# Products with the values issued two quads at a time, with a ring of three probability buffers and v biased in its operand

## The reference

```python
# cross attention, 16 heads of width 16, no scaling of the scores
q = decoded @ Wq.T + bq            # decoded = layernorm(x)
k = encoded @ Wk.T + bk
v = encoded @ Wv.T + bv
qk = einsum('bhqd,bhkd->bhqk', q, k)
attn = softmax(qk, axis=-1)        # nan in qk -> -inf, nan in attn -> 0
v = where(isnan(v), 0, v)
z = einsum('bhqk,bhkd->bhqd', attn, v)
x = x + layernorm(z + decoded) * gamma + beta
# mixture of experts: 8 experts, the best 2 for each row
z = layernorm(layernorm(x)) * ln_g + ln_b
w = top-2 of softmax(z @ rW + rb), normalised
x = x + layernorm(x) + sum over e of w[e] * (gelu(z @ W1[e] + b1[e]) @ W2[e] + b2[e])
```

## Time and profile before

| | us |
|---|---|
| median of three runs | 853.96 (852.0 to 855.2) |
| profiled execution | 848.4 |
| its span in the trace | 846.7 |
| attention pipeline in its steady state | about 55 to 528 of the span |
| PE busy | 752.9 (89%) |
| DVE busy | 655.0 (77%) |
| ACT busy | 534.6 (63%) |
| POOL busy | 553.3 (65%) |

### The profile page before, as it was taken

The page is one execution under the profiler, slowest core; times in us unless marked ns, Lnnn a source line. Parts: engine busy times, 40 slices in busy tenths (PEclk is TensorE's granted clock), DMA queues, the critical chain, the costliest instruction groups (busy, mean ns, idle before and its releaser), DMA issues.

```text
span 846.7 us, 26238 instructions
## 1 busy us (share of the span) xinstructions
PE 752.9 (89%) x8056; PEld 587.9 (69%) x8057; DVE 655.0 (77%) x1827; ACT 534.6 (63%) x1412; POOL 553.3 (65%) x610
## 2 busy tenths in 40 slices
PE   3489999999999999999999997655797798999994
PEld 2356777777777777777777775444686697999994
DVE  7398998998998998998989997993457865555562
ACT  2246787888888888888878885443363354554551
POOL 5424877777778777777778685333655466676773
PEclk9999999999999999999999999755899899999998
DMA  8765576676676676776776766611243233443441
GB/s 208 140 156 120 123 167 151 158 179 155 157 180 152 155 180 140 178 162 149 174 163 152 188 138 168 205 19 52 43 71 44 46 58 65 68 69 51 66 65 18
DMA packets 152791, 104.43 MB, mean 123 GB/s; under 512 B 68656, under 2 KB 147852, under 8 KB 152608
## 3 DMA queue, kind: packets, MB, share of 16 engines
q1 hardware_dynamic: 132598, 77.03, 40.0%
q0 software_dynamic: 11776, 16.15, 11.5%
q10 hardware_dynamic: 8362, 10.57, 4.3%
HBM read 36.65 MB, written 17.33 MB: 64 GB/s over the span
## 4 chain that ended last, share of the span: by engine, by line
PE 74%; DVE 12%; DMA 4%; issue 4%; POOL 3%; ACT 1%; DVEq 1%; ACTq 1%; POOLq 0%; SPq 0%
PE pj L863 10%; PE s_row L967 10%; PE pj L832 9%; PE s_row L877 9%; PE zt L908 9%; PE s_t L896 9%; PE pj L978 5%; PE zt L978 4%; DVE negmax L1332 3%; PE pj L850 3%; DMA q_stack<-q_part 1%; PE tr L916 1%; PE pj L955 1%; PE tr L932 1%; DVE p_t L1337 1%
## 5 line engine op out<-in xcount | busy, mean ns | idle before, releaser
L1332 DVE TENSOR_REDUCE negmax<-s_row 100x1 f32<-100x361 f32 x512 | 251.3, 523 | 30.3 <-PE s_row L877 23.9
L1155 ACT ACTIVATE p_t<-s_t 128x400 f32<-128x400 f32 x384 | 188.6, 501 | 56.4 <-PE s_t L896 50.1
L877 PE MATMUL s_row<-stack_x,q_stack 125*128 125x361 bf16 x512 | 132.3, 320 | 12.2 <-DVE negmax L1332 5.3
L703 POOL DMA_INDIRECT out_x<-index_space,idx_s x57 | 93.2, 1634 | 72.3 <-DVE index_space L1440 35.9
L896 PE MATMUL s_t<-q_stack,stack_x 128*128 128x100 bf16 x1536 | 128.8, 212 | 9.3 <-ACT p_t L1155 8.6
L896 PEld LDWEIGHTS s_t<-q_stack,stack_x 128*128 128x128 bf16 x1536 | 93.4, 99 | 55.4 <-issue 23.1
L967 PE MATMUL s_row<-w_qkv,v_aug 128*128 128x128 f32 x912 | 118.2, 285 | 12.7 <-DVE v_aug L1427 12.6
L967 PEld LDWEIGHTS s_row<-w_qkv,v_aug 128*128 128x128 f32 x912 | 111.9, 200 | 15.8 <-DVE v_aug L1427 14.4
L1337 DVE TENSOR_SCALAR p_t<-p_t 128x1200 f32<-128x1200 f32 x128 | 102.3, 799 | 6.8 <-ACT p_t L1155 5.6
L863 PE MATMUL pj<-w_qkv,ct 128*128 128x256 f32 x384 | 106.4, 400 | 0.2 <-ACT k_rest L1083 0.2
L1141 ACT ACTIVATE w_qkv<-s_row,b_k 128x128 f32<-128x128 f32 x228 | 65.0, 368 | 63.7 <-PE s_row L967 63.6
(11 more groups left out here) (233 smaller groups left out, 1431.9 us busy)
## 6 DMA issues: line engine op xcount, KB each, us to landing
stack_x<-k_part SPq DMA_DIRECT2D x192, 192.0 KB, 3.8
q_stack<-q_part SPq DMA_DIRECT2D x186, 64.0 KB, 2.0
ct<-in_ctx_t SPq DMA_DIRECT2D x32, 361.0 KB, 4.9
stack_x<-in_w ACTq DMA_DIRECT2D x8, 512.0 KB, 6.4
w_s<-in_w ACTq DMA_DIRECT2D x14, 256.0 KB, 3.1
zscr<-zn SPq DMA_DIRECT2D x32, 100.0 KB
z_in<-zscr SPq DMA_DIRECT2D x32, 100.0 KB
zf_d<-zf_s SPq DMA_DIRECT2D x32, 100.0 KB
```

The costliest lines, as they stand in the source:

```text
L703: pool.indirect_dma_start(out_rows[0:n], bass.IndirectOffsetOnAxis(idx_s[:, k.slot:k.slot + 1], 0), ys[:, k.slot, :], None, bounds_check=n ...
L877: nc.tensor.matmul(s_row[h % 2][:, 0:KEYS], q_stack[0:MROW, b.slot, h, :], k_stack[0:MROW, b.slot, h, 0:KEYS], start=True, stop=True).then ...
L1155: nc.scalar.activation(p_t[:, quad % 2, kt, :], s_t[g % 2][:, 0:4 * Q], ACT.Exp).then_inc(exp_done, 1)
L1332: v.tensor_reduce(negmax[:, b.slot, h:h + 1], s_row[h % 2][0:Q, 0:KEYS], AXIS.X, ALU.max, negate=True).then_inc(max_done, 1)
```

## The change

`values` is called twice in a row: quads 0 and 1 together, in slot 0 of the iteration after the batch's own, and quads 2 and 3 together in slot 6. Quad 0 so moves from slot 9 to slot 0, and quad 2 from slot 3 to slot 6; quads 1 and 3 stay. The wait for the guard stands only at the first of a pair, and is for both quads. `p_t` gets a third buffer and the exponentials of a quad wait for the values of the quad three back in place of two back. `v_raw` goes: the bias is added straight into `v_aug` (rows of 16 words, 32 apart) and the cleaning works in place; the wait for the old values of that slot moves from the cleaning to the bias. `ys` moves to `p_t` and small routing tables to `k_rest`, to make room.

```diff
+def ring(b, quad):
+    return (b.slot + quad) % 3
-        v_raw = sb(es, "v_raw", [128, KT * H, DH])
-        p_t = sb(es, "p_t", [128, 2, KT, 4 * Q])
+        p_t = sb(es, "p_t", [128, 3, KT, 4 * Q])
...
-            v_raw[0:Q].rearrange("q n d -> q (n d)"), (LATE, LATE, LATE, 2 * B, 4 * B, 2 * B, 2 * B, (NT - NF) * E, NT - NF))
+            k_rest[0:Q].rearrange("q c k -> q (c k)"), (LATE, LATE, LATE, 2 * B, 4 * B, 2 * B, 2 * B, (NT - NF) * E, NT - NF))
...
-            ys, idx0, idx1, slot_c, second = carve(idx_at, (2 * D, NT, NT, NT, NT))
+            idx0, idx1, slot_c, second = carve(index_space, (NT, NT, NT, NT))
+            ys = p_t[:].rearrange("p r k n -> p (r k n)")[:, 0:2 * D].rearrange("p (s d) -> p s d", s=2)
...
-                    pe.wait_ge(p_ready, G * b.index + quad + 1)
+                    if quad % 2 == 0:
+                        pe.wait_ge(p_ready, G * b.index + quad + 2)
...
-                                                    p_t[0:n, quad % 2, kt, j * Q:j * Q + Q], start=(kt == 0), stop=(kt == KT - 1))
+                                                    p_t[0:n, ring(b, quad), kt, j * Q:j * Q + Q], start=(kt == 0), stop=(kt == KT - 1))
...
-                        if n.valid() and g % KT == 0:
+                        if n.valid() and g in (KT, 3 * KT):
+                            values(n, g // KT - 1)
                             values(n, g // KT)
...
-                        after(act, pv_done, G * b.index + quad - 1)
-                    nc.scalar.activation(p_t[:, quad % 2, kt, :], s_t[g % 2][:, 0:4 * Q], ACT.Exp).then_inc(exp_done, 1)
+                        after(act, pv_done, G * b.index + quad - 2)
+                    nc.scalar.activation(p_t[:, ring(b, quad), kt, :], s_t[g % 2][:, 0:4 * Q], ACT.Exp).then_inc(exp_done, 1)
...
                 def values_biased(b, last):
-                    after(dve, v_ready, b.index)
+                    after(dve, pv_done, G * (b.index - 2))
...
-                        v.tensor_tensor(v_raw[:, 0:2 * H, :].rearrange("p (t h) d -> p t (h d)", t=2), pj[1][:, :].rearrange("p (t n) -> p t n", t=2),
-                                        bias2, ALU.add).then_inc(v01_biased, 1)
+                        v.tensor_tensor(v_aug[:, b.slot, 0:2 * H, 0:DH].rearrange("p (t h) d -> p t h d", t=2),
+                                        pj[1][:, :].rearrange("p (t h d) -> p t h d", t=2, d=DH), bias2, ALU.add).then_inc(v01_biased, 1)
...
                 def values_cleaned(b):
-                    after(dve, pv_done, G * (b.index - 2))
...
-                    v.scalar_tensor_tensor(v_aug[:, b.slot, :, 0:DH], v_raw[:], 0.0, v_raw[:], ALU.max, ALU.min).then_inc(v_ready, 1)
+                    biased = v_aug[:, b.slot, :, 0:DH]
+                    v.scalar_tensor_tensor(biased, biased, 0.0, biased, ALU.max, ALU.min).then_inc(v_ready, 1)
...
-                    v.tensor_scalar(p_t[:, quad % 2], p_t[:, quad % 2], 0.0, None, ALU.max).then_inc(p_ready, 1)
+                    v.tensor_scalar(p_t[:, ring(b, quad)], p_t[:, ring(b, quad)], 0.0, None, ALU.max).then_inc(p_ready, 1)
...
                 def result(k):
...
+                    if k.known and k.index == 0:
+                        dve.wait_ge(pv_done, G * B)
```

More of the change, by code:

```diff
@@ L476, in build @@
             q_stack = sb(att, "q_stack", [128, 3, H, QPAD], BF16)
-            index_space = sb(att, "index_space", [128, KT * D])
+            index_space = sb(att, "index_space", [128, 4 * NT])
             negmax = sb(att, "negmax", [Q, 3, H])
@@ L538, in build @@
             base = per_expert(drow[:])
-            idx_at = index_space
-            ys, idx0, idx1, slot_c, second = carve(idx_at, (2 * D, NT, NT, NT, NT))
-            ys = ys.rearrange("p (s d) -> p s d", s=2)
+            idx0, idx1, slot_c, second = carve(index_space, (NT, NT, NT, NT))
+            ys = p_t[:].rearrange("p r k n -> p (r k n)")[:, 0:2 * D].rearrange("p (s d) -> p s d", s=2)
             idx_t = [idx0, idx1]
@@ L1310, in values_biased @@
                 def values_biased(b, last):
-                    after(dve, v_ready, b.index)
+                    after(dve, pv_done, G * (b.index - 2))
                     if last:
                         dve.wait_ge(v2_done, b.index + 1)
-                        v.tensor_tensor(v_raw[:, 2 * H:3 * H, :].rearrange("p h d -> p (h d)"), pj[0][:, 0:D],
-                                        bv_s[:, :], ALU.add).then_inc(v2_biased, 1)
+                        v.tensor_tensor(v_aug[:, b.slot, 2 * H:3 * H, 0:DH], pj[0][:, 0:D].rearrange("p (h d) -> p h d", d=DH),
+                                        bv_s[:, :].rearrange("p (h d) -> p h d", d=DH), ALU.add).then_inc(v2_biased, 1)
                     else:
                         dve.wait_ge(v01_done, b.index + 1)
-                        bias2 = bv_s[:, :].unsqueeze(1).broadcast_to([128, 2, D])
-                        v.tensor_tensor(v_raw[:, 0:2 * H, :].rearrange("p (t h) d -> p t (h d)", t=2), pj[1][:, :].rearrange("p (t n) -> p t n", t=2),
-                                        bias2, ALU.add).then_inc(v01_biased, 1)
+                        bias2 = bv_s[:, :].rearrange("p (h d) -> p h d", d=DH).unsqueeze(1).broadcast_to([128, 2, H, DH])
+                        v.tensor_tensor(v_aug[:, b.slot, 0:2 * H, 0:DH].rearrange("p (t h) d -> p t h d", t=2),
+                                        pj[1][:, :].rearrange("p (t h d) -> p t h d", t=2, d=DH), bias2, ALU.add).then_inc(v01_biased, 1)
                 def values_cleaned(b):
-                    after(dve, pv_done, G * (b.index - 2))
                     dve.wait_ge(v2_biased, b.index + 1)
                     dve.wait_ge(v01_biased, b.index + 1)
-                    v.scalar_tensor_tensor(v_aug[:, b.slot, :, 0:DH], v_raw[:], 0.0, v_raw[:], ALU.max, ALU.min).then_inc(v_ready, 1)
+                    biased = v_aug[:, b.slot, :, 0:DH]
+                    v.scalar_tensor_tensor(biased, biased, 0.0, biased, ALU.max, ALU.min).then_inc(v_ready, 1)
                 def row_max(b, h):
```

## The result

The changed kernel is slower: 881.68 us in the median of 6 runs (879.68 to 886.24), against 852.98 us (850.0 to 855.84, 6 runs) for the kernel before. The ratio is 1.0349, with a 95% interval of 1.0321 to 1.0376. Predicted were 877.5 us, in a range of 866 to 888. The profiled execution took 881.81 us, with a span of 880.1.

The account below looks back on a forecast made before the run. PE's stream bounds the kernel, but a closed PE-DVE-ACT chain would set the iteration: 28 x 0.82 = 23.0 us plus 0.5 for the tail, 848.4 to 871.9 profiled, so 877.5 us against the 853.96 median; range 866 to 888.

Parts of the forecast that it names:

- the step that was under-sized: Other two iterations of a loop turn: assumed to lose the same 0.82 us as the one worked out.
- What the pairing removes: Values on PE: a lone quad costs 0.76 us, a second one 0.52, so a pair saves 0.24, two 0.48 an iteration.
- First place, head 7: Slot 4: with quad 2 gone from this stretch, PE's row scores of head 7 wait some 0.7 us for maximum 5.
- Second place, step 8: Slot 11: PE waits 0.80 us for exponential 6, with quad 0 gone from slot 9 and the old slot 8 wait gone.
- the second account: Cross-check of an iteration: PE's own work 14.82 us plus waits of 0.70 and 0.80 makes 16.32.
- The sum of an iteration: Closed chain PE to DVE and back twice: legs add to 16.33 us against 15.51, 0.82 more an iteration.
- The signs that I named: Profile after: L1319 repeats every 16.3 us, PE about 92% busy, DVE's idle time up about 0.8 us an iteration.
- The remaining edits at nothing: Guard wait, third buffer, bias with gaps, cleaning in place: taken as 0; bias between -0.05 and +0.1 us an iteration.
- The tail: Last batch: quad 2 right before quad 3 at half clock, last z up to 1.0 us later; taken 0.5, range 0 to 2.
- That no wait takes the place of the saving: Rival: entries and exits are saved without new waits, 14.82 us an iteration, 835 us; chance 0.06.
- that only one does: Rival: only head 7 or only step 8 waits, giving 854 to 857 us; chance 0.05.
- That back to back saves nothing: Rival: the second quad is held up like a lone one, 1.30 us more an iteration, 891 us; chance 0.06.

Follow-up runs that it names:

- Experiments 3 and 6: 3: changed kernel with only quads 2 and 3 paired, 864.03 us; 6: changed kernel with maxima of heads 4 and 5 over 181 of 361 keys, 871.93 us.
- experiment 4: The changed kernel with ACT's copy of the maxima moved from slot 8 to slot 9, behind exponential 6: 872.68 us, ratio 1.0222.
- experiment 1: The changed kernel with the pairing alone undone, the four quads standing one by one again: 853.35 us, ratio 1.0016.
- experiments 2 to 5: Changed kernel with only quads 0 and 1 paired, 862.45 us; only 2 and 3, 864.03; maxima copy in slot 9, 872.68; also z steps in slot 9, 864.71.
- experiments 4 and 5: Changed kernel with ACT's copy of the maxima in slot 9: 872.68 us; the same plus DVE's three z steps in slot 9: 864.71 us.
- both versions of 8 to 11: Quads 1 and 2 paired in slot 3, quad 0 in slot 11: 848.79, 849.83 us; quads 0 and 1 paired, maxima copy and z steps in slot 9: 848.56.
- their control: The version with quads 1 and 2 paired, but quad 1 alone in slot 0 and all other slots the same: 853.25 us, ratio 1.0017.
- experiment 8: The changed kernel with quads 1 and 2 paired in slot 3, quad 0 alone in slot 11, some ACT and POOL steps moved: 848.79 us, ratio 0.9956.

## Why the prediction was right, point by point

The forecast was 23.5 us more, the medians differ by 28.7. The mechanism is the one on record; the sum is short by 5 us, and the point on the step that was under-sized says where.

- **What the pairing removes.** Right. A block of 48 records lasts 1.24 us, to the digit 0.72 + 0.52.
- **First place, head 7.** Right in its mechanism and in when head 7 starts: 0.07 behind maximum 5. Right too in how long PE stands in all: from the scores at 307.84 to the row scores at 308.87 it takes 1.03 us where it took 0.56 (307.24 to 307.80), and 0.24 more inside the pair, together 0.71. Wrong in where: I put it all at the row scores, and most of it went earlier, at the router's transpose (308.46), of which 0.28 is put down to ACT, a wait that I hadn't looked for. It is beside the chain, since head 7 can't start sooner in any case. Experiments 3 and 6 show this leg.
- **Second place, step 8.** Right: 0.54 us idle for exponential 6 (step 8 starts 0.88 us after step 7 where it took 0.18, so 0.70 later in all), and the guard next behind it, as experiment 4 shows. The size I gave, 0.80, took the wait in slot 8 for gone. It grew instead to 0.77 - 0.47 = 0.30 us: the maximum of head 12 now starts late (DVE waits 0.31 us for its row score, at 314.76), and head 15 feels that. It is again beside the chain. Counted from start to start, PE stands 0.71 + 0.30 + 0.70 = 1.71 us in this iteration; the second account had 1.50, for an iteration that turned out 0.27 shorter than this one.
- **The sum of an iteration.** The iteration on which I worked gives 16.33; its fellow in the trace after, the next behind the one shown, takes 340.59 - 324.24 = 16.35. That is no balance of errors, since its legs agree one by one. Head 7 to head 12 is 5.01 us (worked out: 5.00), head 12 to the end of exponential 6 is 3.71 (3.73), and from there to the values it is 0.34 (0.32). Head 12, step 8 and the start of its wait are in these rows:

```profile
330.88 0.47 PE L880 MATMUL s_row<-stack_x,q_stack 125*128 125x361 bf16 x2
...
334.65 0.35 PE L899 MATMUL s_t<-q_stack,stack_x 128*128 128x100 bf16 x4 [0.42 <-ACT p_t L1160]
```

- **The signs that I named.** L1324 repeats every 16.48 us in the mean, as forecast to 0.2. PE's busy share is 94.1 to 94.6%, not 92 (and the prediction's own terms, 14.82 of 16.33, would make 91); why it is higher isn't shown. DVE's idle time grew from 9.4% of 15.65 us to 12.7% of 16.6, which is 0.6 us an iteration and not 0.8.
- **The step that was under-sized** is "I take the same difference for them", for the other two iterations of a loop turn. A turn took 337.63 - 290.69 = 46.94 us before and takes 340.59 - 290.75 = 49.84 now, 0.97 an iteration. These are the starts, of the kernel before and then of the changed one:

```profile
290.69 0.69 DVE L1319 TENSOR_TENSOR v_raw<-pj,bv_s 128x512 f32<-128x512 f32 x1 [0.36 <-PE pj L863]
...
337.63 0.69 DVE L1319 TENSOR_TENSOR v_raw<-pj,bv_s 128x512 f32<-128x512 f32 x1 [0.36 <-PE pj L863]
```

```profile
290.75 0.69 DVE L1324 TENSOR_TENSOR v_aug<-pj,bv_s 128x512 f32<-128x512 f32 x1 [0.36 <-PE pj L866]
...
340.59 0.69 DVE L1324 TENSOR_TENSOR v_aug<-pj,bv_s 128x512 f32<-128x512 f32 x1 [0.36 <-PE pj L866]
```

I had picked the iteration with most slack. In the one before it exponential 6 ended later against step 8; this row of ACT and this of PE are from the kernel before:

```profile
300.27 0.51 ACT L1155 ACTIVATE p_t<-s_t 128x400 f32<-128x400 f32 x1
```

```profile
301.14 0.72 PE L908 MATMUL zt<-p_t,v_aug 128*32 128x100 f32 x24
```

  Exponential 6 ends at 300.78, and step 8 starts 0.27 before the values, at 300.87: 0.09 us of room, against 0.22 in the iteration I used. So the chain of this iteration comes out 0.13 longer against what PE took, 0.95 us more; it took 1.03 more (324.24 - 307.62 = 16.62, before 306.28 - 290.69 = 15.59). The third iteration has the loop's branch. It stands in front of the values of slot 0, and now also right behind a wait. Before the change:

```profile
331.26 0.50 ACT L1155 ACTIVATE p_t<-s_t 128x400 f32<-128x400 f32 x1
```

```profile
331.70 0.52 PE L896 MATMUL s_t<-q_stack,stack_x 128*128 128x100 bf16 x8
332.31 0.91 PE L908 MATMUL zt<-p_t,v_aug 128*32 128x100 f32 x24
333.14 0.35 PE L896 MATMUL s_t<-q_stack,stack_x 128*128 128x100 bf16 x4
```

  And in the changed kernel:

```profile
301.27 0.35 PE L899 MATMUL s_t<-q_stack,stack_x 128*128 128x100 bf16 x4 [0.52 <-ACT p_t L1160]
301.97 1.24 PE L912 MATMUL zt<-p_t,v_aug 128*32 128x100 f32 x48 [0.35 <-issue]
```

  The room was small here too: exponential 6 ended at 331.76, and step 8, the second four of the eight, started at 331.88, 0.12 later, so 0.10 less room than in the iteration I used. This iteration took 15.84 us before and takes 307.62 - 290.75 = 16.87. The branch itself is not new. From step 7 to the scores behind the values PE took 333.14 - 331.70 = 1.44 us, against 317.30 - 316.20 = 1.10 in the iteration I used, so it cost 0.34 already; now step 8 to the values takes 0.70 in place of 0.28, so 0.42. Of the 0.1 us an iteration that I had kept for it at the end of the range, 0.08 came, once in three. So a turn is 2.90 us longer: three times 0.82 is 2.46, the smaller room of two iterations 0.23, the branch 0.08, and 0.13 stays open.
- **Over the whole kernel.** From the first L1324 to the last, the kernel with the pairing undone takes 531.6 - 46.9 = 484.7 us and the changed one 558.4 - 47.5 = 510.9. So 26.2 of the 28.7 us between the medians lie in these 31 intervals, 0.85 us each. The turn shown has 0.97 each; the other intervals have less in the mean. I had counted 28 iterations at 0.82, 23.0 us.
- **The remaining edits at nothing.** Right, by experiment 1. The bias takes 691 ns with gaps in its rows, as it did without.
- **The tail.** From the last L1324 to the end the trace after takes 880.1 - 558.4 = 321.7 us and before 846.7 - 528.3 = 318.4. The kernel with the pairing undone has 852.3 - 531.6 = 320.7, so about 1 us of the difference is the pairing's, within what single executions differ by. The first start of this line comes 4.5 us later than before (47.5 against 43.0). In the edited kernels it comes at 44.5 to 49.0, in no order with the edits. The one profile of the kernel before is the earliest of all, but the kernel with the pairing undone starts at 46.9 and has the time of the kernel before (1.0016), so I don't count these 4.5 us as the pairing's.
- **Rivals.** That no wait takes the place of the saving, and that only one does, are out by experiments 2 to 5. That back to back saves nothing is out by the block's 1.24 us.

## What to carry to other kernels

When one engine is 99% busy and its partner 90%, follow single dependencies round one iteration before believing that work removed is time saved: add up, leg by leg, what each partner takes from the work that it waits for to the work that waits for it. Work that is moved out of such a leg on the busy engine was its cover, and work that is moved into the leg's front delays everything behind it; both were so here, and the sum of the legs gave the loss of the iteration that it was worked on within a few per cent (0.82 us, measured 0.84). Taken over to the other two it was too small (0.82, measured 1.03). Do this for each iteration of an unrolled turn, not for one, and when the chain closes, look at whether the partner's own order can be shortened: two steps moved on ACT and DVE turned the same pair from 1.2% slower into 0.4% faster.

## What the runs showed that I had not expected

- The loop's branch on PE, once a turn, cost 0.34 us already before the change and 0.42 in the changed kernel, as the rows above show, and the iteration with it took 15.84 us where the others took 15.59 and 15.51. In experiments 4 and 5, in both versions of 8 to 11 and in their control that iteration is no longer than the others: 16.18 beside 16.31 and 16.09, 15.76 beside 15.87 and 15.76, 15.51 beside 15.59 and 15.51 in the control. In the kernels where the branch costs time, step 8, the last work in front of it, starts in that iteration 0.12 us or less after exponential 6; where it costs nothing, step 8 starts 0.3 us or more after it. So the branch seems to be hidden when PE has not just been held up in front of it. No run varies this alone.
- The same subtraction on POOL (`m_low`, 100 x 16) took 0.75 us in the kernel before and 0.87 or 1.56 in the version with quads 1 and 2 together, where it runs at another moment. The row of the latter:

```profile
302.15 1.56 POOL L744 TENSOR_TENSOR m_rows<-m_rest,m_rows 100x16 bf16<-100x16 f32 x1 [0.33 <-ACT m_rows L1216]
```

  It ends at 303.71. Beside it on DVE the cleaning of `v_aug` runs from 302.00 to 302.94 and a guard from 302.86 to 303.64. In the kernel before it ends at 302.35 + 0.75 = 303.10, and a guard at 302.11 + 0.93 = 303.04. So it goes through both traces: apart from one or two of them near the start, which take 0.22 us, each ends 0.06 to 0.09 us after a guard or a cleaning on DVE that ran while it did. This looks as if the small step on POOL had to wait inside its own time for the DVE work beside it, which would also make the wait of the transpose in experiment 8. No experiment moves one against the other, so it is not shown as the cause.
